# Two score products of 59 rows in two row groups of the array, and value products in two halves

## The reference

```python
h = _layernorm(x) * (1 + ca) + sa
q = einsum('bsd,hde->bhse', h, wq) + bq          # k and v alike; 16 heads of 8
scores = softmax(einsum('bhse,bhte->bhst', q, k) * scale, axis=-1)
att = einsum('bhst,bhte->bhse', scores, v)       # joined over the heads
x = x + ga * (att @ wo.T + bo)
...                                              # experts of layer 0, then layer 1
```

## Time and profile before

| | |
|---|---|
| median of 3 runs | 1227.03 us (1226.36 to 1229.6) |
| the profiled execution | 1232.33 us, its span 1230.7 us |
| PE busy | 1016.2 us (83%) |
| DVE busy | 760.8 us (62%) |
| ACT busy | 590.8 us (48%) |
| POOL busy | 447.9 us (36%) |
| S maxima (DVE L634) | 512, 324.5 us busy, 683 ns each |
| exponentials (ACT L528) | 512, 287.0 us busy, 597 ns each |
| value products (PE L821) | 1024, 612 ns each, four at a time |

### The profile page before, as it was taken

How to read it: one execution, slowest core, us unless ns; L and a number is a source line. 1 busy time by engine, 2 the same in 40 slices (tenths; PEclk the granted TensorE clock), 3 DMA queues, 4 the chain that set the end, 5 groups by cost and what they waited for, 6 DMA issues and landing times.

```text
span 1230.7 us, 21656 instructions
## 1 busy us (share of the span) xinstructions
PE 1016.2 (83%) x6352; PEld 655.6 (53%) x6352; DVE 760.8 (62%) x1940; ACT 590.8 (48%) x1257; POOL 447.9 (36%) x631
## 2 busy tenths in 40 slices
PE   4699999999999999941788887887878788887992
PEld 3132333332333333321777777776777778787771
DVE  3668887877888788870667464444545555454562
ACT  1057676766677767721234241423414364454551
POOL 4030414131313131212244344543543336545673
PEclk9579999999999999975989788888989879897996
DMA  4442516060605153306000000100000112112332
GB/s 132 135 136 56 169 32 185 17 191 12 190 20 180 57 153 129 101 9 264 18 18 19 18 19 18 31 18 22 17 18 18 36 34 57 48 48 89 111 99 68
DMA packets 57727, 92.14 MB, mean 75 GB/s; under 512 B 9658, under 2 KB 41576, under 8 KB 56982
## 3 DMA queue, kind: packets, MB, share of 16 engines
q1 hardware_dynamic: 46806, 59.09, 16.7%
q0 software_dynamic: 10816, 31.84, 7.3%
HBM read 50.02 MB, written 41.29 MB: 74 GB/s over the span
## 4 chain that ended last, share of the span: by engine, by line
PE 31%; DVE 6%; another core or an unknown queue 6%; issue 5%; ACT 3%; POOL 2%; DMA 1%; DVEq 0%; ACTq 0%; POOLq 0%; SPq 0%
PE a L2158 5%; PE a L2147 5%; PE tb L1971 4%; PE a L1963 4%; PE a L1981 3%; PE b_ L1937 2%; PE c L1937 2%; DMA xg<-tokens_dram,row_of 1%; PE b_ L1932 1%; ACT weights L1544 1%; PE tb L2139 1%; PE b_ L2025 1%; POOL xg L1300 1%; ACT L1495 1%
## 5 line engine op out<-in xcount | busy, mean ns | idle before, releaser
L634 DVE TENSOR_REDUCE nmax<-ps_s 128x1 f32<-128x512 f32 x512 | 324.5, 683 | 84.4 <-PE ps_s L799 83.2
L528 ACT ACTIVATE p_ring<-ps_t 128x512 f32<-128x512 f32 x512 | 287.0, 597 | 138.3 <-PE ps_t L810 134.7
L821 PE MATMUL ps_av<-p_ring,v_ext 128*32 128x512 f32 x1024 | 137.9, 612 | 0.0
L1313 POOL DMA_INDIRECT back_dram<-weights,target x78 | 87.4, 1121 | 98.6 <-DVE weights L1881 78.2
L799 PE MATMUL ps_s<-weights 72*128 72x512 bf16 x256 | 107.4, 423 | 18.9 <-DMA weights<-q_parts_dram 15.5
L1544 ACT ACTIVATE weights<-a,wtile 128x128 f32<-128x128 f32 x312 | 89.2, 372 | 65.2 <-PE a L2147 58.1
L1451 ACT ACTIVATE hid<-a 128x512 f32<-128x512 f32 x64 | 38.2, 597 | 170.6 <-PE a L1963 109.1
L2147 PE MATMUL a<-hTt,wtile 128*128 128x128 f32 x624 | 91.6, 294 | 18.2 <-issue 12.6
L2158 PE MATMUL a<-wtile,weights 128*128 128x128 f32 x624 | 91.1, 293 | 14.8 <-ACT weights L1544 9.0
L810 PE MATMUL ps_t<-weights 75*128 75x512 bf16 x256 | 101.0, 394 | 2.8 <-ACT p_ring L528 1.7
L810 PE MATMUL ps_t<-q_stack,k_stack 75*128 75x512 bf16 x256 | 96.7, 382 | 3.9 <-ACT p_ring L528 2.0
(11 more groups left out here) (280 smaller groups left out, 1690.6 us busy)
## 6 DMA issues: line engine op xcount, KB each, us to landing
rows_dram<-wmod POOLq DMA_DIRECT2D x8, 2340.0 KB
q_parts_dram<-q_parts SPq DMA_DIRECT2D x40, 128.0 KB, 2.3
xt<-rows_dram SPq DMA_DIRECT2D x78, 65.0 KB
weights<-k_parts_dram SPq DMA_DIRECT2D x16, 288.0 KB
weights<-q_parts_dram SPq DMA_DIRECT2D x16, 288.0 KB
k_stack<-k_parts_dram SPq DMA_DIRECT2D x16, 288.0 KB
q_stack<-q_parts_dram SPq DMA_DIRECT2D x16, 288.0 KB
wall<-in_wall SPq DMA_DIRECT2D x1, 4112.0 KB, 20.4
```

What stands on the lines that cost most here:

```text
L528: nc.scalar.activation(probs[:, u % RING, :], ps_t[u % TBANKS][:], ACT.Exp, scale=HD ** -0.5).then_inc(exp_done, 1)
L634: nc.vector.tensor_reduce(nmax[:, js, n:n + 1], ps_s[u % SBANKS][:], AX.X, ALU.max, negate=True).then_inc(max_done, 1)
L821: last = nc.tensor.matmul(ps_av[32 * g:32 * (g + 1), :], v_ext[par][:, t, HG * j + g, :], probs[:, (HG * k + g) % RING, :], start=(t == 0) ...
L1313: nc.gpsimd.indirect_dma_start(out=scratch["back"].ap(), out_offset=bass.IndirectOffsetOnAxis(ap=target[j % YT][:, 0:1], axis=0), in_=yt[j ...
```

## The change

The two smallest of the nine products of parts are left out, so that 7 x 8 = 56 rows and the three of the maxima fit in 64. Heads stand in two row groups, at partitions 0 and 64 (`place_in_stack`): in each block of four heads two are in the lower and two in the upper. The S products take the heads in the order 2, 3, 0, 1 (`head_of_score`), the T products 0, 1, 2, 3, so that a unit's S and T product are in different row groups. The value products come in two halves of 256 columns, after the second and the fourth unit of a group. The stacks are loaded in two lots for two blocks of heads each, eight transfers a lot, and the columns of wq and wk are put in the new order on the host. `k_stack` is filled with ones by POOL at the start, in place of two transfers from `ones`; the stacks no longer lie in `weights0`. A maximum's block moves in two transfers. Layer 1, its rows in two lists included, is the same in both.

```diff
-STACK = TERMS * HD
+Q_SLOTS = (0, 1, 2, 0)
+WIDE, NARROW = 2 * HD * PARTS, HD
+STACK = WIDE + NARROW
+GROUP = 64
+HGROUP = P // GROUP
...
+def head_of_score(v):
+    return (v + 2) % HG
+def place_in_stack(j, g):
+    per = HG // HGROUP
+    return GROUP * (g // per), per * j + g % per
...
-            def load_stacks(j, par):
-                n = HG * T
-                sp.dma_start(k_stack[par][0:STACK, HG * j:HG * (j + 1), :],
-                             window(scratch["k"], n * j, [[H * T, PARTS * HD], [0, PARTS], [1, n]])
-                             ).then_inc(stack_in[j], 16)
-                sp.dma_start(q_stack[par][0:STACK, HG * j:HG * (j + 1), :],
-                             window(scratch["q"], n * j, [[H * T, PARTS * HD], [HD * H * T, PARTS], [1, n]])
-                             ).then_inc(stack_in[j], 16)
+            def load_stacks(i, par):
+                n = NG // 2 * (HG // HGROUP)
+                for rg in range(HGROUP):
+                    row, first = GROUP * rg, H // HGROUP * rg + n * i
+                    here = slice(n * i, n * (i + 1))
+                    for stack, dram, step, last in ((k_stack, "k", 0, 2), (q_stack, "q", HD * H * T, 0)):
+                        sp.dma_start(stack[par][row:row + WIDE, here, :],
+                                     window(scratch[dram], T * first, [[H * T, 2 * HD], [step, PARTS], [1, n * T]])
+                                     ).then_inc(stack_in[i], 16)
+                        sp.dma_start(stack[par][row + WIDE:row + STACK, here, :],
+                                     window(scratch[dram], T * first + last * HD * H * T, [[H * T, HD], [1, n * T]])
+                                     ).then_inc(stack_in[i], 16)
...
                     load_stacks(0, 1 - par)
-                    load_stacks(1, 1 - par)
...
                 if it.after:
-                    load_stacks(2, 1 - par)
-                    load_stacks(3, 1 - par)
+                    load_stacks(1, 1 - par)
...
-            nc.gpsimd.memset(ones[:], 1.0).then_inc(consts, 1)
             nc.gpsimd.memset(half[:], -0.5).then_inc(consts, 1)
             for i in range(2):
+                nc.gpsimd.memset(k_stack[i][:], 1.0).then_inc(consts, 1)
+            for i in range(2):
                 nc.gpsimd.memset(v_ext[i][:], 0.0).then_inc(consts, 1)
...
             def score(bs, js, v, u, par):
-                if v == 0:
-                    pe.wait_ge(stack_in[js], 32 * (bs + 1))
+                if v == 0 and js % 2 == 0:
+                    pe.wait_ge(stack_in[js // 2], 16 * 4 * HGROUP * (bs + 1))
...
-                nc.tensor.matmul(ps_s[u % SBANKS][:], q_stack[par][0:STACK, h, quarter(t)], k_stack[par][0:STACK, h, :],
-                                 start=True, stop=True).then_inc(s_filled, 1)
+                row, c = place_in_stack(js, head_of_score(v))
+                nc.tensor.matmul(ps_s[u % SBANKS][:], q_stack[par][row:row + STACK, c, quarter(t)],
+                                 k_stack[par][row:row + STACK, c, :], start=True, stop=True).then_inc(s_filled, 1)
...
+                some = slice(T // 2 * i, T // 2 * (i + 1))
                 for g in range(HG):
-                    last = nc.tensor.matmul(ps_av[32 * g:32 * (g + 1), :], v_ext[par][:, t, HG * j + g, :],
-                                            probs[:, (HG * k + g) % RING, :], start=(t == 0), stop=(t == NT - 1))
-                last.then_inc(av_done, 1)
+                    last = nc.tensor.matmul(ps_av[32 * g:32 * (g + 1), some], v_ext[par][:, t, HG * j + g, :],
+                                            probs[:, (HG * k + g) % RING, some], start=(t == 0 and i == 0),
+                                            stop=(t == NT - 1), skip_group_check=True)
+                if i:
+                    last.then_inc(av_done, 1)
...
-                    if u == HG - 1 and it.before:
-                        weigh(prev, H - 1, 1 - par)
-                    elif u % HG == HG - 1 and u >= HG and it.here:
-                        weigh(b, u // HG - 1, par)
+                    if u % HG in (1, 3):
+                        if u < HG and it.before:
+                            weigh(prev, H - 1, 1 - par, u % HG // 2)
+                        elif u >= HG and it.here:
+                            weigh(b, u // HG - 1, par, u % HG // 2)
```

More of the change, by code:

```diff
@@ L121, in take_best, with stack_heads @@
                             imm_value=-1.0).then_inc(taken, 1)
+def head_of_score(v):
+    return (v + 2) % HG
+def stack_heads():
+    per = HG // HGROUP
+    return [HG * j + per * rg + i for rg in range(HGROUP) for j in range(NG) for i in range(per)]
+def place_in_stack(j, g):
+    per = HG // HGROUP
+    return GROUP * (g // per), per * j + g % per
 def scores_of(u, it):
@@ L172, in program_attention @@
         ident_b = sb("ident_b", [P, P], BF16)
[L173 removed]
         half = sb("half", [P, NT])
[L176 to L178 removed]
+        q_stack = [sb(f"q_stack{i}", [P, H // HGROUP, T], BF16) for i in range(2)]
+        k_stack = [sb(f"k_stack{i}", [P, H // HGROUP, T], BF16) for i in range(2)]
         v_ext = [sb(f"v_ext{i}", [P, NT, H, 32]) for i in range(2)]
@@ L264, in program_attention @@
         k_saved = sem("k_saved")
-        stack_in = [sem(f"stack_in{j}") for j in range(NG)]
+        stack_in = [sem(f"stack_in{i}") for i in range(2)]
         s_filled = sem("s_filled")
@@ L346, in _ @@
             sp.dma_start(x_all[:, 1:B], io["x"][1:B].rearrange("b (t p) d -> p b t d", p=P)).then_inc(x_in, 16)
-            sp.wait_ge(consts, 1)
-            for i in range(2):
-                sp.dma_start(k_stack[i][MROW:MROW + PARTS], ones[:]).then_inc(ones_in, 16)
             def move_maxima(bb, j, par):
                 sp.wait_ge(m_rows_ready[j], bb + 1)
-                sp.dma_start(q_stack[par][MROW:MROW + PARTS, HG * j:HG * (j + 1), :],
-                             m_rows[:, j, :]).then_inc(m_in[j], 16)
+                n = PARTS * HG * NT // HGROUP
+                for rg in range(HGROUP):
+                    row, column = place_in_stack(j, HG // HGROUP * rg)
+                    sp.dma_start(q_stack[par][row + MROW:row + MROW + PARTS, column:column + HG // HGROUP, :],
+                                 m_rows[n * rg:n * (rg + 1), j, :]).then_inc(m_in[j], 16)
             def save_parts(parts, ready, saved, dram, slots, bb):
-                for j in range(NG):
-                    sp.wait_ge(stack_in[j], 32 * bb)
+                for i in range(2):
+                    sp.wait_ge(stack_in[i], 16 * 4 * HGROUP * bb)
                     settle(sp)
@@ L392, in iteration @@
                 if it.after:
-                    save_parts(k_parts, (k1_ready, k2_ready, k3_ready), k_saved, scratch["k"], PARTS, nxt)
-                    save_parts(q_parts, (q1_ready, q2_ready, q3_ready), q_saved, scratch["q"], QSLOTS, nxt)
+                    save_parts(k_parts, (k1_ready, k2_ready, k3_ready), k_saved, scratch["k"], range(PARTS), nxt)
+                    save_parts(q_parts, (q1_ready, q2_ready, q3_ready), q_saved, scratch["q"], Q_SLOTS, nxt)
+                    if not it.here:
+                        sp.wait_ge(consts, 3)
                     if it.before:
@@ L804, in score_t, with weigh @@
                 if u % (HG * NT) == 0:
-                    pe.wait_ge(m_in[j], 16 * (b + 1))
-                    pe.wait_ge(ones_in, 32)
+                    pe.wait_ge(m_in[j], 16 * HGROUP * (b + 1))
                 if u >= TBANKS or not (isinstance(b, int) and b == 0):
                     pe.wait_ge(exp_done, UNITS * b + u - units_back(u, TBANKS) + 1)
-                h = HG * j + g
-                nc.tensor.matmul(ps_t[u % TBANKS][:], k_stack[par][0:STACK + PARTS, h, quarter(t)],
-                                 q_stack[par][0:STACK + PARTS, h, :], start=True, stop=True).then_inc(t_filled, 1)
-            def weigh(b, k, par):
+                row, c = place_in_stack(j, g)
+                rows_ = slice(row, row + STACK + PARTS)
+                nc.tensor.matmul(ps_t[u % TBANKS][:], k_stack[par][rows_, c, quarter(t)], q_stack[par][rows_, c, :],
+                                 start=True, stop=True).then_inc(t_filled, 1)
+            def weigh(b, k, par, i):
                 j, t = k // NT, k % NT
```

58 lines of the change are left out of this document (30 added, 28 removed).

## The result

The change takes 1212.17 us (median of 20 runs, 1206.36 to 1228.4) against 1226.6 for the kernel before beside it: ratio 0.9873, 95% interval 0.9853 to 0.9892, so 14.4 us faster. The two slowest of its runs, 1224.74 and 1228.4 us at a lower clock, are left out of the ratio. A gain of 48 was forecast. The profiled execution took 1214.23 us, its span 1212.5.

The account below looks back on a forecast made before the run. TensorE's serial order was taken to bound the steady part, VectorE next. Start 4.0, iteration 0 -7, six iterations -6 x 6.8, iteration 7 -4.5: -48.3 us, from 1227.0 to 1179; own range 1152 to 1206, stated 1152 to 1218.

Parts of the forecast that it names:

- two rivals that did not come about: Weight loads not hidden under products (1215 us, chance 0.08); loads landing 3 us late for unit 32 (1200 us, chance 0.08).
- Pairs and halves: TensorE in attention: S and T products together at 0.22 us, half the value products 0.55; TensorE alone 2.18 a group.
- A group: Four units of the attention loop, with waits for ScalarE: 2.5 us in place of 3.11; sixteen groups save 9.8 an iteration.
- Weights exposed: Rival: weights cannot load under a running product of the same row group, 0.10 us more a unit; 1215 us, chance 0.08.
- The loads: Eight transfers for groups 0 and 1 take 7.9 us and land about a microsecond before unit 32 needs them.
- The start: Two POOL fills of 3.6 us each delay the first normalisation to 12.1; 4.0 us lost in all.
- Iteration 0: First attention iteration: no gain in 16.2 us at half clock, 7 us gained in the other 44.9.
- Iteration 7: Last attention iteration, scores in its first half alone: 4.5 us gained.
- What comes back: Per iteration, 1.2 us returns as wait at the normalisation chain and 1.8 through VectorE's side work; 52.0 us results.
- 6 x 6.8: Six like middle iterations of attention, each 6.8 us shorter, from 58.8 to 52.0.
- The clock stays down: Rival: TensorE, again waiting for VectorE, loses its full clock; a group takes 4.2 us, time over 1300, chance 0.04.
- clock 0.5 inside the iterations: Sign that the forecast is wrong: TensorE's clock at 0.5 within the attention iterations.

Follow-up runs that it names:

- Same rows: The changed kernel with S products taking heads in the T products' order, so a pair shares a row group; four runs, 1280.37 to 1398.85 us (before 1228.35).
- whole products: The changed kernel with value products whole again, 512 columns after each fourth unit; 1205.38 us, ratio 0.9824 to the kernel before.
- both readers halved: The changed kernel with VectorE's maxima and ScalarE's exponentials each over half their data, part of the computation left out; 1176.14 us (before 1213.83).
- the early normalisation: The changed kernel with the normalisation of the sequence after next moved half an iteration earlier; 1209.43 us, ratio 0.9853 to the kernel before.

## Why the prediction was wrong

The direction was right, and so was the mechanism of the pair. The gain was less than a third of the forecast. The time lies in the stated 1152 to 1218, but above 1206, where the forecast's own range ended; what lay above had been added for two rivals that did not come about. Step by step:

- **Pairs and halves**: right. 0.22 a pair, 0.57 a half (0.55), TensorE alone 2.22 a group (2.18). The Trainium skill (TensorE: Matmul & The Clock Gate, Part 3), which has products in different row groups start some 4 ns apart, agrees with the trace, which has them within 10 ns.
- **A group**: too short. Four units without other products take 2.8 in the mean, beyond the 2.5 taken and its bound of 2.7.
- **Weights exposed**: refuted. Pairs follow one another at 0.22 in the same row groups.
- **The loads**: right. The first lot takes 44.95 - 37.07 = 7.9, as forecast, and no score in the loop waits for a load.
- **The start**: right. Fills of 3.5 us each, normalisation at 12.03 (12.1); 3.4 lost to the first exponential (4.0). Moving the fills gives it back.
- **Iteration 0**: 7.4 less (7), by luck. All of the 7 was to come from its 44.9 us at full clock and nothing from the 16.2 at half clock. In the trace its first 16 units are 3.5 shorter, where the clock rises 8.9 us after the first exponential in place of 15.8, and the other 48 only 3.9. The row also shows TensorE busy for 15.4 of the 16.2 us, so that stretch was not spent waiting on the chain.
- **Iteration 7**: 2.2 less (4.5).
- **"What comes back", and with it "6 x 6.8"**: wrong; this is the step that failed. I let 3.0 of the 9.8 us come back, to 52.0, kept the 9.0 us of TensorE's other products at their price, and put six like iterations into the sum, so that the loop's jump and falls of the clock stood at nothing. An iteration with full clock measures 55.9, beyond the bound of 55.5, so 6.9 came back; and the six iterations together lose another 10 at the loop's jump and by the clock. 348.4 - 355.8 = -7.4 stands where -41 was forecast. This is nearly the whole miss; the parts that were measured add up to 3.4 - 7.4 - 7.4 - 2.2 = -13.6.

What was in place of 3.0, first in an iteration with full clock, 3.9 us above the forecast:

- *TensorE's other products got dearer, about 2.3.* I took the 9.0 us of them as they were; it was the rest of 58.8 after sixteen groups of 3.11. Counted from start to start, the 64 products into `bank_a` and `bank_b` took 8.75 us in the iteration of the earlier trace rows, and 10.62 in those of after at full clock; some entries are 0.32 for 0.22 besides. Same rows and whole products have 10.6 too, the kernel before with halves 9.0. So it comes neither with the concurrency nor with the halves, but with the score products of 56 and 59 rows in two row groups; no run parts their height from their place. The Trainium skill (TensorEngine Tiling (Array Packing), Key Properties) says that a change of tiling mode drains the engine. The trace agrees, if the half-height products count as another mode, and gives the price: 0.10 on entering and 0.14 on leaving. By rows alone, it is 0.32 and 0.58 where it was 0.22 and 0.44.
- *Work in the groups, 0.6, and waits, 1.0.* TensorE's own work is now 16 x 2.22 + 10.62 + 0.7 for entries (seven that follow a T product, 0.10 each), about 46.8, so 9.1 of 55.9 are waits. By the same count the forecast held 16 x 2.18 + 9.0 = 43.9 of work and 8.1 of waits. So 2.9 of the 3.9 us are TensorE's work, and only 1.0 are waits beyond those that I had allowed. Where they stand is shown above: 3.0 for ScalarE, 2.9 for VectorE and 1.8 for POOL are the largest. With both readers halved, T products start 0.4 and S products 0.9 us late in the iteration at full clock, and the wait for POOL is 2.0; the early normalisation gains 0.8 at full clock. I had VectorE's slack spread over the iteration and a quarter of its side work in the way. The runs show that both readers cost, about alike, and one at a time: where TensorE must go in order through S, T, value and other products with three and two banks, each late bank stops all that is behind it.

And over the six iterations 10 more, which the forecast had at nothing:

- *The loop's jump, 5.5.* The last four units of iteration 3 take 10.6 us, where in an undisturbed iteration they take 3.8; before the change 4.5 and 3.2. Halves and loop together make the gap of 7.0; without either of them it is absent. The instruction queue shows that with halves the loop's code is fetched a second time; that TensorE waits for it in its two idle times is read from the times.
- *The clock, 4.2.* It fell at the fronts of iterations 2, 3 and 6, and they lost 1.6, 2.9 and 1.3 us there; before, only iteration 4 lost 1.6 so, just behind the jump. It fell behind the longer wait for POOL, not every time, and without that wait it didn't.

My rival "The clock stays down" looked for a clock lost for good. What came was a fall of 3.4 to 6.8 us at three fronts and of 10.2 at the jump, which I had not priced, though "clock 0.5 inside the iterations" was one of my signs of being wrong. Of the range's lower end, an iteration of 48.2, no run came near, even with both readers halved.

## What to carry to other kernels

A saving in one engine's steady group is worth its length only in stretches where that engine alone sets the pace; here dearer work between the groups and the waits for the two readers and at the iteration's front took back seven of ten microseconds. When products change their height and place in the array, price each change of shape in the loop, not only the products that change. Splitting instructions in a long loop body can cost at the jump, where more code has to be fetched again: try each part of a change alone, since here the pairs carried all of the gain and the halves none.

## What the runs showed of the hardware

- Between products of 56 or 59 rows in two row groups and f32 products of 128 rows and 128 columns each crossing took 0.10 to 0.14 us more than with products of 72 and 75 rows, also when no two products ran side by side. To the value products of 32 columns each it took 0.30 to 0.32 in both kernels.
- A fill of 4096 bf16 elements took 3.5 us on POOL and one of 2048 f32, as many bytes, 1.88: the element counts, not the byte.
- TensorE stood for 4.64 and 2.37 us at the loop's jump, for 6.46 in the kernel before with halves, and not at all with whole products. The queue of its code moved 12, 11 and 1 packets from 285 to 425 us in these three.
- TensorE's clock fell to its lower level behind a wait of 1.7 us at an iteration's front in three iterations, for 3.4 to 6.8 us, and in two others it did not. Before the change the same front, with waits of 0.8 to 0.9, kept it; the one fall in these iterations came just behind the loop's jump.
